# Edge walk of a graph layer: the next turn's node-block number is loaded behind the product, not in front of the message

## The reference, cut to what matters

```
q, k, v = x@Wq + bq, x@Wk + bk, x@Wv + bv          # 8 heads of 32
logits  = einsum('ehd,ehd->eh', q[dst], k[src]) / sqrt(32)
seg_max = segment_max(logits, dst)
expv    = exp(logits - seg_max[dst])
attn    = expv / segment_sum(expv, dst)[dst]
agg     = segment_sum(attn[:, :, None] * v[src], dst)
```

## Time and profile before

| | us |
|---|---|
| median of 3 runs | 4355.9 (4355.7 to 4357.51) |
| span of the profiled execution | 4355.3 |
| PE busy | 3439.8 (79%) |
| DVE busy | 3480.0 (80%) |
| ACT busy | 2533.3 (58%) |
| POOL busy | 2677.3 (61%) |

### The profile page before, as it was taken

One profiled execution on the slowest core, in us unless ns is written; L12 is line 12 of the kernel. 1 busy time (PEld: TensorE's weight loads), 2 busy tenths in 40 slices (PEclk: granted clock), 3 DMA queues, 4 the chain that ended last, 5 costly groups with the idle time before them and its releaser, 6 DMA issues. The chain is left out here.

```text
span 4355.3 us, 107023 instructions
## 1 busy us (share of the span) xinstructions
PE 3439.8 (79%) x26106; PEld 2517.5 (58%) x26107; DVE 3480.0 (80%) x9712; ACT 2533.3 (58%) x6256; POOL 2677.3 (61%) x2719
## 2 busy tenths in 40 slices
PE   7887988889898988989898888248888888887620
PEld 3335777777777777777777676235555555555410
DVE  8887988889898988989898898866666666666457
ACT  5436766767676766767676676545555555555310
POOL 3226766666666666666666663227777777777740
PEclk9988999999999999999999999559999999999855
DMA  6537777767677767777776774611121111111147
GB/s 222 182 118 231 227 212 220 212 210 227 207 226 215 224 208 214 227 212 218 217 225 207 215 225 152 215 56 26 30 35 31 31 30 31 31 35 30 22 95 274
DMA packets 367763, 677.61 MB, mean 156 GB/s; under 512 B 70294, under 2 KB 240482, under 8 KB 367074
## 3 DMA queue, kind: packets, MB, share of 16 engines
q0 software_dynamic: 157888, 420.64, 35.2%
q1 hardware_dynamic: 183106, 223.48, 15.2%
q10 hardware_dynamic: 26080, 25.70, 2.0%
HBM read 582.00 MB, written 87.58 MB: 154 GB/s over the span
## 5 line engine op out<-in xcount | busy, mean ns | idle before, releaser
L742 POOL DMA_INDIRECT KV<-kv_d,src_i x1564 | 1558.6, 997 | 775.9 <-issue 437.0
L1385 POOL DMA_INDIRECT re_src<-src_tab_d,rsrc x1024 | 985.9, 963 | 312.1 <-issue 245.6
L1011 PE MATMUL agg_ps<-msg,oh 128*128 128x264 f32 x3512 | 865.2, 390 | 2.5 <-DVE msg L837 1.9
L837 DVE TENSOR_TENSOR msg<-KV,msg 128x1024 f32<-128x1024 f32 x439 | 537.9, 1225 | 225.1 <-issue 223.9
L1011 PEld LDWEIGHTS agg_ps<-msg,oh 128*128 128x128 f32 x3512 | 640.4, 192 | 98.8 <-ACT oh L926 2.0
L969 PE MATMUL Q<-q,ohT 128*128 128x256 bf16 x5328 | 672.4, 277 | 1.9 <-issue 0.9
L911 ACT ACTIVATE square<-iota_b,off 128x128 bf16<-128x128 bf16 x1784 | 569.4, 392 | 0.3
L845 DVE TENSOR_TENSOR prod<-KV,Q 128x1024 f32<-128x1024 f32 x443 | 537.8, 1214 | 5.1 <-POOLq L733 3.4
L849 DVE TENSOR_REDUCE lg<-prod 128x32 f32<-128x1024 f32 x443 | 535.0, 1208 | 0.2
L969 PEld LDWEIGHTS Q<-q,ohT 128*128 128x128 bf16 x5328 | 495.7, 99 | 64.2 <-issue 2.2
L922 ACT ACTIVATE msg<-dl 128x32 f32<-128x32 f32 x439 | 113.4, 258 | 662.3 <-DVE dl L807 662.3
(11 more groups left out here) (261 smaller groups left out, 5864.4 us busy)
## 6 DMA issues: line engine op xcount, KB each, us to landing
q<-q_d SPq DMA_DIRECT2D x446, 192.0 KB
y_d<-ex_y ACTq DMA_DIRECT2D x56, 448.0 KB
rg_ye<-y_d SPq DMA_DIRECT2D x7, 3584.0 KB, 12.5
KV<-kv_d,src_i POOLq DMA_INDIRECT x1564
nu_xs<-xs_d SPq DMA_DIRECT2D x7, 2688.0 KB, 11.7
re_src<-src_tab_d,rsrc POOLq DMA_INDIRECT x1024
kv_d<-pr_kv SPq DMA_DIRECT2D x49, 256.0 KB, 2.2
xs_d<-pr_xs SPq DMA_DIRECT2D x49, 256.0 KB, 2.3
```

What stands on the lines that cost most here:

```text
L742: pool.indirect_dma_start(out=KV[:, t % (KVR * G), :], out_offset=None, in_=k.kv_d, in_offset=bass.IndirectOffsetOnAxis(ap=k.src_i[:, t:t ...
L837: v.tensor_tensor(m[:, :, :, 0:DH], KV[:, tiles(s), D:2 * D].rearrange("p t (h d) -> p t h d", d=DH), bc(m[:, :, :, DH:HW], [P, G, HEADS, ...
L1011: pe.matmul(agg_ps[:, 0:HEADS * HW], oh32[ring(s, 2)][:, t, :], msg[ring(s, 2)][:, t, :, :].rearrange("p h e -> p (h e)"), start=(t == 0), ...
L1385: pool.indirect_dma_start(out=gs[:, t % (RING * RG), :], out_offset=None, in_=k.src_tab_d, in_offset=bass.IndirectOffsetOnAxis(ap=k.rsrc[: ...
```

## The change

The call `window(s + 1)` moves from its place in front of `message(s - 1)` to the place behind `product(s + 4)`, in front of `scale_sums(s - 1)`. It is the only edit. No instruction is added or taken out of a turn, and no other engine's stream differs.

```diff
                     if there(s):
                         raise_max(s)
-                    if there(s) and not last:
-                        window(s + 1)
                     if there(s + (-1)):
                         message(s + (-1))
                     if there(s):
                         fall(s)
                     product(s + 4)
+                    if there(s) and not last:
+                        window(s + 1)
                     if there(s + (-1)):
                         scale_sums(s + (-1))
                     logits(s + 4)
```

## The result

The changed kernel takes 4284.8 us (median of 4 runs, 4283.5 to 4288.9); the kernel before took 4356.7 beside it. The ratio is 0.983, with a 95% interval of 0.982 to 0.985: faster by 72 us, where 169 were forecast. That lies outside the stated range of 4155 to 4225 us. In a second comparison the same kernel gave 0.984 (0.982 to 0.985).

The account below looks back on a forecast made before the run. VectorE was taken as the bound. 166 us from the gap before the message plus 3 us at the heads of passes made 169 off the 4355.3 us span: 4186, plus 0.6 for the median, 4187 us; range 4155 to 4225.

Parts of the forecast that it names:

- The gap in front of the message: VectorE's idle time before the message, caused by the block-number load; removing it saves 0.39 us in 425 turns, 166 us.
- the turn with GpSimd at rest, 0.50: Last turns of a pass load nothing ahead; five, with GpSimd standing still, were 0.50 us shorter, partly not the load's.
- the one with 0.38: Last turn of a pass without the load, 4.66 us against 5.04; basis for the 0.39 us taken per turn.
- The excess at fixed places: Turns at fixed places idle 0.5 to 0.8 us instead of 0.42, some 17 us in all; not counted as gain.
- The load behind the product: Moved load between product and `scaled`, covered by the product's 1.13 us: costed at nothing; uncovered, 0.65 us in full.
- The first rival: Load exposed behind the product, leaving a gap before `scaled`: 110 us lost, 4466 us; slower was given 0.04.
- TensorE late next: TensorE needs 4.66 us a turn against VectorE's new 4.72, so it is only 0.06 us short of being the bound.
- stays ahead: GpSimd waits up to 5.04 us about once in nine turns, which become 3.5 us shorter, so it isn't the bound.
- The rival in which GpSimd becomes the bound: Denser VectorE slows each of 1564 gathers 0.1 us; the walk shrinks 135 us at most: 4221 us; half of 0.12.
- the trace shows 0.1: Gathers take 0.95 us, some 1.05; this 0.1 us was set against the skill's full lock on the shared port.
- A gather would be held for the message's 1.2 us: What a full lock of the port shared by VectorE and GpSimd would do to a gather, by the Trainium skill.

Follow-up runs that it names:

- two halves: The changed kernel with its message instruction split into two instructions of four heads each: 4161.7 us, ratio 0.956; a second time 4163.7 us, 0.956.

## Why the prediction was wrong

Point by point, by its own steps.

**The gap in front of the message: right.** The message starts 0.09 us behind `m_new`, the idle time there is gone save at the heads of the passes, and VectorE's free turn is 4.65 us, where 4.72 was given. The turn fell by 5.11 - 4.65 = 0.46. It was the turn with GpSimd at rest, 0.50, that foretold it better than the one with 0.38. The excess at fixed places (17 us), which I left where it is, went too. VectorE's side of the sum was thus too small, not too large: on the pages the idle time in front of the message fell from 225.1 to 26.8, by 198 us, and the run with a quarter of the gathers left out gained 195. With GpSimd out of the way the forecast would thus have been some 26 us too small a gain, within its range.

**The load behind the product: right.** `scaled` follows the product with no idle time except in the first turn of a pass, where I had given 0.3 us of lateness for the second load:

```profile
1124.11 1.23 DVE L837 TENSOR_TENSOR msg<-KV,msg 128x1024 f32<-128x1024 f32 x1 [0.79 <-issue]
1125.33 1.21 DVE L845 TENSOR_TENSOR prod<-KV,Q 128x1024 f32<-128x1024 f32 x1
1126.84 0.43 DVE L832 TENSOR_TENSOR scaled<-acc,fac 128x264 f32<-128x264 f32 x1 [0.30 <-issue]
```

The message of that turn waits 0.79 us in place of 1.48, 0.7 earlier where I gave 0.6. The first rival, the one that would have made the kernel slower, did not occur.

**TensorE late next: nearly, but it never became the bound.** It needs 4.64 us a turn where 4.66 was worked out from the earlier trace rows, against VectorE's 4.65; in every kernel here it starts most of its turns 0.15 us behind `running`. What came up to VectorE besides was ScalarE, which the prediction checked by its idle time and not by when its weights are due. They were ready 0.6 us before the message; in the changed kernel it is 0.15 us, for the message of 1228.57:

```profile
1228.16 0.26 ACT L922 ACTIVATE msg<-dl 128x32 f32<-128x32 f32 x1 [0.93 <-DVE dl L807]
```

No message of any run starts less than 0.14 us behind its weights. More taken out in front of the message would thus gain nothing unless the weights came earlier, which no run tried. The 41.4 us for which VectorE waits for queries are there in the changed kernel and in no list of waits with a quarter of the gathers left out, with two halves or with the weights in PSUM, so they follow from the stalls that GpSimd causes.

**GpSimd: the step that failed.** The prediction held that it "stays ahead", from its waits of up to 5.04 us against 3.5 us less in nine turns, with the gathers as they were. The rival in which GpSimd becomes the bound was named, and its price was wrong by most of its size: 1564 gathers at 0.1 us each, 4221 and 6 in 100. The runs show some 0.9 us for about one gather in five, 225 us more in all than before, and 4285. The 0.1 was no measure of how strongly the two touch. It was the overlap of one particular phase: a gather held for the last tenth of a message. In the earlier trace rows the hold could be read, had the start of that gather been laid beside the message: it started 1.0 us into it and ended 0.1 late, just when a full hold would let it go. And 59 gathers of that trace, 43 of them the fourth behind a wait for the ring, when GpSimd is off its usual phase, took 1.4 to 1.98 us; I did not look at them. The one behind the second row starts 0.49 us into the message of 1197.39:

```profile
1197.88 1.55 POOL L742 DMA_INDIRECT KV<-kv_d,src_i  x1 [0.30 <-issue]
```

What the prediction cited and set aside was the better guide. The Trainium skill (SBUF — State Buffer, SBUF: two separate sides) says that a VectorE instruction with two SBUF inputs and a GpSimd instruction that reads SBUF lock each other out for the whole length of an instruction. I set it aside with "the trace shows 0.1". By that rule, a hold is as long as the rest of the message from where the gather starts, and the traces agree for starts from 0.1 to 1.1 us into it; the run with the weights in PSUM agrees as well. The other half of the rule, the VectorE instruction locked out by a gather that runs already, does not show: the messages that began over a running gather were neither late nor longer. "A gather would be held for the message's 1.2 us" was also a misreading of it, since only the rest of the message can hold one.

**The sum, as it should have been.** This is worked out with the result known. Nine turns hold some 32 gathers. At 1.25 us they need 40 us of the 9 x 4.65 = 41.9 that VectorE leaves. If one gather in each turn starts at 0.2 us into the message, up to nine holds of 0.9 are to be added, 8.1 us, and GpSimd needs up to 48; it becomes the bound, and then its starts drift off that place and some turns escape. In the traces it is GpSimd's own time that counts: from the start of the first gather to that of the last 2329 us before, of which 292 are waits for the message, which leaves 2037; in the changed kernel 2264 us with no such wait. The holds make up the difference of 227, and 2329 - 2264 = 65 us are the gain.

## What to carry to other kernels

Idle time on the bound engine may be what lets another engine in. Before taking it away, look at the engine behind it with the new period: how many of its steps fit one turn, at which point of the turn each starts, and which of the bound engine's instructions it can't start in. A small mean excess of an instruction may be a large one at a lucky phase, so plot its duration over where it starts before pricing it; and where a long instruction holds a neighbour, cutting it in two can be worth more than it costs, but only if that neighbour is the bound.

## What the runs showed of the hardware

VectorE and GpSimd don't meet only through semaphores. A gather that GpSimd starts while VectorE runs an instruction with both inputs in SBUF is held until that instruction ends, 0.90 us for a start at 0.2 of 1.14; one that has started before it is not (0.94 us at 1186.79 in the kernel before), and doesn't hold the instruction up either. An instruction of the same length with one input in PSUM holds none (0.94 or 0.95 us for all 299 that start inside it). A register load costs VectorE's sequencer about 0.6 us, of which 0.34 to 0.42 show on the engine when only short instructions are queued ahead of it, and nothing when a product of 1.13 us is (a second load behind the same product shows 0.30).
